# Attention pairs on one core: the second unit's normalisation after the opening, two more maximum jobs in the opening, rows loaded quad by quad

## The reference

```python
q, k, v = x @ wq.T, x @ wk.T, x @ wv.T
q, k = _apply_rope_full(q), _apply_rope_full(k)          # over the whole width
q, k, v = (t.reshape(B, S, 16, 8).transpose(0, 2, 1, 3) for t in (q, k, v))
scores = jnp.einsum('bhqd,bhkd->bhqk', q, k) / math.sqrt(8)
scores = scores + _alibi_slopes(16)[None, :, None, None] * rel[None, None]
scores = jnp.where(causal[None, None], jnp.float32(-1000000000.0), scores)
out = jnp.einsum('bhqk,bhkd->bhqd', jax.nn.softmax(scores, -1), v)
# x = x + _L0_attn_ref(_layernorm(x), ...)
```

## Time and profile before

| what | value |
| --- | --- |
| three timed runs | 1323.32, 1326.98, 1327.03 us; median 1326.98 us |
| the profiled execution: its own time | 1324.17 us |
| its span, first to last instruction | 1322.4 us |
| mean granted TensorE clock | 0.989 of full speed |

### The profile page before, as it was taken

The page is one execution under the profiler, slowest core; times in us unless marked ns, Lnnn a source line. Parts: engine busy times, 40 slices in busy tenths (PEclk is TensorE's granted clock), DMA queues, the critical chain, the costliest instruction groups (busy, mean ns, idle before and its releaser), DMA issues.

```text
span 1322.4 us, 17165 instructions
## 1 busy us (share of the span) xinstructions
PE 1220.3 (92%) x6083; PEld 784.8 (59%) x6132; DVE 906.3 (69%) x1754; ACT 641.6 (49%) x1188; POOL 241.4 (18%) x205
## 2 busy tenths in 40 slices
PE   5998788899899989899999969889998998999998
PEld 3676444567666555566667744346776665555665
DVE  6755867455467698986765677664555677889765
ACT  4544354544422597952234325454433227979222
POOL 3000100000020084751000010000000102938210
PEclk9999899999999999999999999999999999999999
DMA  6212220000101030320100032200001011212220
GB/s 231 57 33 80 56 76 19 2 1 1 64 1 64 4 118 23 116 81 1 73 25 1 24 89 54 63 3 0 1 1 64 16 50 58 81 58 80 65 72 9
DMA packets 33365, 63.27 MB, mean 48 GB/s; under 512 B 4384, under 2 KB 20096, under 8 KB 33088
## 3 DMA queue, kind: packets, MB, share of 16 engines
q1 hardware_dynamic: 33280, 62.17, 15.0%
HBM read 54.23 MB, written 8.45 MB: 47 GB/s over the span
## 4 chain that ended last, share of the span: by engine, by line
PE 72%; DVE 11%; ACT 9%; issue 3%; POOL 2%; DMA 2%; SPq 1%; another core or an unknown queue 0%; DVEq 0%; POOLq 0%; ACTq 0%
PE bank L1543 13%; PE bank L1545 13%; PE bank L1544 13%; PE bank L1722 9%; PE bank L1552 5%; DVE a_mx L1426 3%; ACT n_part L1093 3%; PE bank L1877 3%; PE bank L1621 3%; ACT n_da L1085 2%; PE bank L1787 2%; PE bank L1692 2%; POOL n_hc L840 2%; PE bank L1758 2%; PE bank L1826 1%
## 5 line engine op out<-in xcount | busy, mean ns | idle before, releaser
L1270 DVE SCALAR_TENSOR_TENSOR f_hl<-bank,f_hh 128x512 fp32r<-128x512 f32 x192 | 131.9, 689 | 130.4 <-ACT f_hh L914 129.6
L914 ACT ACTIVATE f_hh<-bank 128x512 fp32r<-128x512 f32 x192 | 115.0, 599 | 188.1 <-PE bank L1621 149.2
L980 ACT ACTIVATE m_sl<-bank 128x512 f32<-128x512 f32 x144 | 86.2, 599 | 235.4 <-PE bank L1545 233.4
L840 POOL TENSOR_TENSOR n_hc<-n_h,n_cs 128x512 f32<-128x512 f32 x128 | 160.7, 1287 | 35.3 <-DVE n_h L1514 31.1
L1543 PE MATMUL bank<-xT_h,mw_h 128*128 128x512 f32 x288 | 161.2, 560 | 3.5 <-DVEq L537 2.7
L1514 DVE TENSOR_TENSOR_SCAN n_h<-n_da,bank 128x512 f32<-128x512 f32 x128 | 149.1, 1206 | 5.1 <-PE bank L1552 2.3
L1722 PE MATMUL bank<-m_h,mw 128*128 128x512 f32 x288 | 145.6, 594 | 0.0
L1337 DVE TENSOR_TENSOR m_t<-m_sl,bank 128x512 f32<-128x512 f32 x128 | 87.9, 687 | 78.7 <-PE bank L1545 77.3
L1426 DVE TENSOR_REDUCE a_mx<-bank 128x1 f32<-128x384 f32 (+3 forms) x176 | 106.0, 638 | 39.8 <-PE bank L1828 37.4
L771 POOL TENSOR_TENSOR small<-small,half 128x4 f32<-128x4 f32 (+1 forms) x24 | 26.8, 1115 | 577.3 <-DVE small L1176 577.3
L1877 PE MATMUL bank<-n_hc,ident 128*128 128x512 f32 x256 | 131.0, 599 | 0.2
(11 more groups left out here) (248 smaller groups left out, 2331.1 us busy)
## 6 DMA issues: line engine op xcount, KB each, us to landing
n_cs<-c_dram SPq DMA_DIRECT2D x32, 512.0 KB, 3.6
m_c<-comb_dram SPq DMA_DIRECT2D x28, 512.0 KB, 5.2
stage_fw<-in_fw_dram SPq DMA_DIRECT2D x6, 512.0 KB, 6.4
stack_dram<-R SPq DMA_DIRECT2D x16, 192.0 KB, 2.8
w_stage<-in_mw_dram SPq DMA_DIRECT2D x9, 256.0 KB, 2.7
stack_dram<-R SPq DMA_DIRECT2D x16, 128.0 KB, 2.6
a_q<-stack_dram SPq DMA_DIRECT2D x4, 512.0 KB, 5.3
a_k<-stack_dram SPq DMA_DIRECT2D x8, 256.0 KB, 4.7
```

The lines of the kernel that those rows point to most:

```text
L840: n_hcs.by(nc.gpsimd.tensor_tensor(n_hc[:, i % 4, :], n_h[:, i % 4, :], n_cs[:, j % C_RING, i // 2 % 2, :], ALU.mult))
L1270: f_lo.by(V.scalar_tensor_tensor(f_h[1][:, i % 4, :], bank[:, i % 3, :], 0.0, f_h[0][:, i % 4, :].bitcast(F32), ALU.max, ALU.subtract))
```

## The change

1. `plan[-1]` takes 10 instead of 8 jobs behind `vals`: 20 of the first unit's 44 maximum jobs stand in the opening instead of 18. The first unit's remaining jobs and turns come one or two steps earlier: its turns stand at steps 3, 11 and 17 (4, 12 and 19 before).
2. The second unit's jobs run from step 20 (19 before); their last one stands in step 51 (49 before) and its turns in steps 29, 37, 45 and 51.
3. `HEAD_LAG[0]` is -4: the stages of the second unit's prologue stand two score steps later. Stages 0, 2, 4, 5 and 6 (statistics, rows, transposition, high and low part), which stood in the opening, are called behind the opening, at step 0, at step 1 and in the loop.
4. Four loads of rows, one for each quad, instead of three. Where load 0 stood, loads 0 and 1 stand.
5. GpSimd computes the second unit's inverse root after the copies of the first unit's values, not before them.

```diff
@@ -61,8 +61,8 @@
 
     plan = {step: [] for step in range(-1, 2 * NS2 + 1)}
     first, second = maxima(0), maxima(1)
-    plan[-1] = first[:NS1] + [("vals", 0, 0)] + first[NS1:NS1 + 8]
-    first = first[NS1 + 8:]
+    plan[-1] = first[:NS1] + [("vals", 0, 0)] + first[NS1:NS1 + 10]
+    first = first[NS1 + 10:]
     for step in range(2 * NS2):
         count = int(1.5 * (step + 1)) - int(1.5 * step)
         plan[step] += first[:count]
@@ -87,7 +87,7 @@
 
 
 NEXT_VALUES = 12
-NEXT_MAXIMA = [(19, 51, 1.5)]
+NEXT_MAXIMA = [(20, 52, 1.5)]
 HEADS_PLAN = heads_plan()
 
 
@@ -127,7 +127,7 @@
 HEAD_PARTS = [f"{side} {c}" for side in "qk" for c in range(3)]
 HEAD_ROTATIONS = ["first", "second", "k first", "k second"]
 HEAD_RESIDUALS = ["third", "fourth", "k rest", "k last"]
-HEAD_LAG = {0: -6, 1: 11}
+HEAD_LAG = {0: -4, 1: 11}
 KEYS_LATER = 2
 
 
@@ -441,8 +441,8 @@
         a_vok = sig("a_vok", "mha", 2)
         a_fin = sig("a_fin", "mha", 1)
         a_wr = sig("a_wr", "mha", 12, 16)
-        a_ldq = [sig(f"a_ldq_{n}", "mha", 1, 16) for n in range(3)]
-        a_ldk = [sig(f"a_ldk_{n}", "mha", 2, 16) for n in range(3)]
+        a_ldq = [sig(f"a_ldq_{n}", "mha", 1, 16) for n in range(QUADS)]
+        a_ldk = [sig(f"a_ldk_{n}", "mha", 2, 16) for n in range(QUADS)]
         a_rld = sig("a_rld", "pair", 1, 16)
         a_s1 = sig("a_s1", "mha", QUADS * NS1)
         a_m1 = sig("a_m1", "mha", QUADS * NS1)
@@ -598,7 +598,7 @@
                 sp.wait_ge(a_prt.sem, a_prt.at(k, 3 * side + 2))
                 if k % 2 == 1:
 
-                    for n in range(3):
+                    for n in range(QUADS):
                         sp.wait_ge(a_ldq[n].sem, a_ldq[n].at(k - 1, 0))
                         sp.wait_ge(a_ldk[n].sem, a_ldk[n].at(k - 1, 1))
                 for slot, n, part in PART_RUNS:
@@ -610,7 +610,7 @@
 
             def head_rows_in(k, n):
 
-                first, count = ((0, 4), (4, 2), (6, 2))[n]
+                first, count = 2 * n, 2
                 to = slice(first % 4, first % 4 + count)
                 sp.wait_ge(a_wr.sem, a_wr.at(k, 5))
                 a_ldq[n].by(sp.dma_start(a_qs[first // 4][:, to],
@@ -693,13 +693,14 @@
                     if p == 0:
 
                         sp.wait_ge(unit_done, done_before(u))
-                        head_rows_in(k, 1)
                         head_rows_in(k, 2)
+                        head_rows_in(k, 3)
                     for quad in range(QUADS):
                         if p == 0 and quad == 3:
 
                             sp.wait_ge(a_s2.sem, a_s2.at(k, NS2 // 2 - 1))
                             head_rows_in(k + 1, 0)
+                            head_rows_in(k + 1, 1)
                         sp.wait_ge(a_mok.sem, a_mok.at(k, quad))
                         if p == 1:
 
@@ -715,11 +716,11 @@
                         if p == 0 and quad == QUADS - 1:
 
                             sp.wait_ge(a_s2.sem, a_s2.at(k, 3 * STEPS_4 - 1))
-                            head_rows_in(k + 1, 1)
+                            head_rows_in(k + 1, 2)
                         if p == 1 and quad == 0:
 
                             sp.wait_ge(a_s2.sem, a_s2.at(k - 1, NS2 - 1))
-                            head_rows_in(k, 2)
+                            head_rows_in(k, 3)
                 if kind == "ffn" and u + 1 < NU and UNITS[u + 1][0] == "mha":
                     k = kth[u + 1]
                     a_rld.by(sp.dma_start(rope[:], A["rope"]))
@@ -729,6 +730,7 @@
                         sp.wait_ge(w_lo.sem, w_lo.at(0, len(SPLITS) - 1))
                     head_rows(k, 1)
                     head_rows_in(k, 0)
+                    head_rows_in(k, 1)
                 if kind == "mamba":
                     state_rows(k)
                 if u + 1 < NU and UNITS[u + 1][0] == "moe":
@@ -810,7 +812,6 @@
                     if p == 0:
                         blank(k // 2, 1)
                         a_fill.by(nc.gpsimd.memset(a_v[:, :, :, DH:32], 1.0))
-                        prologue(u + 1, "guess")
                     pool.wait_ge(a_vst.sem, a_vst.at(k, 0))
                     for n, heads in enumerate((slice(0, 12), slice(12, 16))):
                         if p == 1:
@@ -818,8 +819,7 @@
                             pool.wait_ge(a_pv.sem, a_pv.at(k - 1, (11, 15)[n]))
                         a_vok.by(nc.gpsimd.tensor_copy(
                             a_v[:, :, heads, 0:DH], a_vs[:].rearrange("p t (h d) -> p t h d", d=DH)[:, :, heads]))
-                    if p == 1:
-                        prologue(u + 1, "guess")
+                    prologue(u + 1, "guess")
                 if kind == "mamba":
                     if p == 0:
                         n_fill.by(nc.gpsimd.memset(n_xp[:, :, 0:3], 0.0))
@@ -987,7 +987,6 @@
                 if p == 0:
                     for job, x, n in HEADS_PLAN[-1]:
                         head_job(k, job, n)
-                    hand_over(u, 5)
                 for s_ in range(NS2):
                     at = NS2 * p + s_
                     w = T - s_ // 2 % NT * P
@@ -1366,17 +1365,15 @@
 
                 b = batch_of(u)
                 if p == 0:
-                    for n, (job, x, which) in enumerate(HEADS_PLAN[-1]):
+                    for job, x, which in HEADS_PLAN[-1]:
                         head_job(k, job, which, b)
-                        if n == NS1 - 1:
-                            hand_over(u, 0)
-                        if n == NS1 + 3:
-                            hand_over(u, 2)
-                    hand_over(u, 6)
+                    hand_over(u, 0)
                 V.tensor_tensor(X[:, b], X[:, b], out_b[:].unsqueeze(1).to_broadcast([P, NT, P]), ALU.add)
                 for s_ in range(NS2):
                     for job, x, which in HEADS_PLAN[NS2 * p + s_]:
                         head_job(k - p + x, job, which, b - p + x)
+                    if p == 0 and s_ == 0:
+                        hand_over(u, 2)
                     if s_ >= HEAD_LAG[p] and s_ >= 1:
                         hand_over(u, s_ - HEAD_LAG[p])
             def normalise(k, g):
@@ -1741,7 +1738,6 @@
                     ready(u)
                     for job, x, which in HEADS_PLAN[-1]:
                         head_job(k, job, which)
-                    hand_over(u, 4)
                 for s_ in range(NS2 + 3 * p):
                     at = NS2 * p + s_
                     if s_ < NS2:
@@ -1768,6 +1764,8 @@
                             head_job(k - p + x, job, which)
                     if at >= 3 and at % 2 == 1:
                         weigh_heads(k - p, (at - 3) // 2)
+                    if p == 0 and s_ == 1:
+                        hand_over(u, 4)
                     if s_ > HEAD_LAG[p] and 1 <= s_ < NS2:
                         hand_over(u, s_ - HEAD_LAG[p])
             def weigh_heads(k, tile):
@@ -1790,7 +1788,7 @@
 
             def rows_of_quads(k, n):
 
-                pe.wait_ge(a_fill.sem, a_fill.at(k // 2, 1 if n == 0 else 3))
+                pe.wait_ge(a_fill.sem, a_fill.at(k // 2, 1 if n < 2 else 3))
                 pe.wait_ge(a_ldq[n].sem, a_ldq[n].at(k, 0))
                 pe.wait_ge(a_ldk[n].sem, a_ldk[n].at(k, 1))
 
@@ -1817,8 +1815,8 @@
                 if job == "slot":
 
                     quad, (qt, h0, nh) = n // NS1, SLOTS_4[n % NS1]
-                    if n % NS1 == 0 and quad != 1:
-                        rows_of_quads(k, max(quad - 1, 0))
+                    if n % NS1 == 0:
+                        rows_of_quads(k, quad)
                     w = (qt + 1) * P
                     last = bank[:, b, 0:nh * w].rearrange("p (h w) -> p h w", w=w)[:, :, qt * P:w]
                     for c in range(nh):
```

## The result

The changed kernel takes 1330.92 us in the median of six runs (1329.63 to 1332.84); the kernel before, in its six runs, 1325.76 us (1323.32 to 1327.03). The ratio is 1.0041, 95% interval 1.0031 to 1.0051: 5.4 us slower, 4.1 to 6.8. I forecast slower by 2.4 us. The profiled execution took 1331.07 us with a span of 1329.3 us, so 6.9 us more than the one before; 1.3 us of these lie ahead of the first pair, where the two programs are the same (TensorE's last products there begin at 130.25 instead of 128.93), and are no effect of the change. (The pair's first maximum job stands at 132.76 for 131.68, 1.1 us later: the other 0.2 us are won at the pair's first load, as forecast.)

The account below looks back on a forecast made before the run. TensorE was taken as the bound (busy 92%, 72% of the chain), so only its waits in the two attention pairs pay. 2 x (2.2 - 0.9) - 0.2 = +2.4 us gave 1329.4 us on the median 1326.98; range 1322 to 1334.

Parts of the forecast that it names:

- Opening: Pair's start: step 0 begins 2.3 us earlier, at 145.0, but PE then waits 1.5 us before the transposition.
- The rows' chain: Second unit's rows: ACT's copy ends 2.3 us later, at 175.0; rows land at 184.6, 1.2 us later than before.
- step 12: End of dense steps 3 to 11: begins at 167.6, 0.2 us ahead; bounds 1.6 ahead to 0.7 behind.
- Rival D: Second unit's key load: halving it saves nothing, rows land 1.2 us later than forecast, +2.4 us, 1331.8; chance 0.10.
- What it has done ahead is that product, which before ran slow: At the wait for the second unit's rows: values product and step 20's scores already done, PE 0.9 us ahead.
- The price behind it: After the second unit's rows land: left-over jobs, waits at steps 32 and 40, later turns; 2.2 us behind per pair.
- a quad's parts fall into step 43, where the next unit's statistics begin: 0.3: Second unit's end: 1.0 us of VectorE parts of the maxima meet the next unit's statistics, costing 0.3 us.
- Quad 3's maxima: On SP's queue: they queue behind two loads and land some 2 us before step 24.
- A: The forecast itself, every step a row's duration: own range 1327 to 1332; chance 0.40.
- B: Steps 32, 40, 48, 56: PE waits 1.9, 1.3, 0 and 0.5 us for maxima rows; +6.2 us, 1333.2; chance 0.20.
- C: Second unit's rows not late: copy only 0.9 us later, PE 2.3 ahead; faster, about 1323.5; chance 0.20.
- E: Whole kernel: the change moves nothing, waits trade places one for one, 1327.0; chance 0.10.

Follow-up runs that it names:

- e8: e1 with the second unit's normalisation behind the opening, its stages two steps later and the later root (parts 3 and 5 added): 1330.42 us.
- e1: The kernel before with part 4 alone, four loads of rows, one for each quad: 1319.23 us.
- e5: The changed kernel with part 4 undone, so load 0 brings quads 0 and 1 again: 1334.77 us.
- e13: e1 with the keys' last residuals and parts two steps earlier (KEYS_LATER 0 instead of 2): 6.5 us slower than e1.
- e9: e1 with 6 instead of 8 jobs in the opening: 1331.18 us.

## Why the prediction was right in sign and too small

**Opening: right.** Step 0 at 145.0 (145.2 on before's clock), gated by the maxima rows; 1.5 us ahead of the transposition (1.48); "lent, not earned": the 1.9 and 1.5 us of step 0 have shrunk to 0.6 and 0.8 by step 16 and are worth nothing by themselves, as e8 shows.

**The rows' chain: right in kind, short by 0.9 us.** I had ACT's last part at 175.0 and it ended at 175.9; hence the landing 185.5 and not 184.6. The load was 3.47 us for 3.5 forecast, the wait of 2.37 for 2.6, the last turn's 1.92 for 1.9. The failing term is step 12, which I put 0.2 ahead of before; it began at 168.5, 0.7 behind, which was the far end that I had given for it. Rival D is out: the loads here took 3.47 us (3.21 in e1) against 4.57, and undoing the smaller loads in e5 costs 3.8 us. D rested on the fixed cost of about 2 us that the Trainium skill states, page "DMA: Bandwidth & Descriptors", section "Latency and other measured facts". The two times don't contradict such a cost, only what was concluded from it: if 256 KB take 4.57 us and 128 KB 3.47, a straight line through both leaves 2.4 us that do not shrink and 2.2 that halve (an estimate; the query load in front of the key load was halved with it, so the key load's own bytes are not tried alone).

**"What it has done ahead is that product, which before ran slow": wrong.** I counted the slow stretch behind the wait as something that the product could be moved out of. The stretch came behind the wait and then covered other work: 5.66 us at 0.50 instead of 3.2. At step 24 the first pair is 1.2 us behind where I had it 0.9 ahead with 0.5 us of jobs left over; of these 1.6 us about 0.9 are the late rows. The rest is of the size that 2.5 us more at half rate make; no run takes the stretch away by itself. In the second pair, where the stretch is as long before as after, step 24 is 1.3 us ahead, more than I had. What I had missed altogether is how much the wait was worth with its clock: e1 won 7.1 us where I expected 2.4.

**The price behind it: mis-sized in both directions.** I gave 0.5 + 1.1 + 0.5 - 0.6 us to jobs left over, steps 32 and 40 and the early turns, in sum 1.5. Steps 24 to 40 cost 0.2. The wait at step 32 was about 0.6 and at step 40 there was none; and besides the turns' 0.50 us, of which I had counted 0.3, two waits of 0.44 us (at 203.55 and 215.22 before) shrank to 0.21, at which I had not looked. Against this I gave 0.3 us to step 43 and 0.4 to the last turn, and steps 40 to 56 cost 2.6 and 3.8: the term "a quad's parts fall into step 43, where the next unit's statistics begin: 0.3" is the one that failed. VectorE there:

```profile
226.18 0.17 DVE L1433 CAST a_mp<-a_mx 128x16 bf16<-128x16 f32 x1
...
226.86 0.86 DVE L1156 BATCH_NORM_STATS2 st<-X 128x6 f32<-128x128 f32 x4
...
231.21 1.12 DVE L1185 TENSOR_SCALAR xn<-X,mv,small 128x128 f32<-128x128 f32 x4
...
237.22 0.68 DVE L1192 SCALAR_TENSOR_TENSOR xT_l<-bank,xT_h 128x512 fp32r<-128x512 f32 x1
```

Parts of the maxima until 226.35, statistics from 226.86, rows of the normalisation from 231.21 and the low part at 237.22, each ahead of a reduction that holds a bank. PE waits 1.25 us for the one, 1.16 for the next, and 0.52 for the low part, where before one wait of 1.22 us stands: 1.7 us more, and the last turn 0.7: together 2.4 of the 2.6 us of the first pair. The second pair's 1.2 us more stand beside the low clock behind the last turn. I had priced the VectorE work that is added (1.0 us of parts), and not that the jobs run two steps further into the next unit's normalisation, where each instruction of it stands between two reductions.

**Quad 3's maxima.** They queue behind two loads, as I said; I had them land some 2 us ahead of step 24. SP issued (times of the queue):

```profile
185.91 0.56 SPq L708 DMA_DIRECT2D max_dram<-R  x1
189.32 1.50 SPq L712 DMA_DIRECT2D a_q<-max_dram  x2
```

3.41 us between the write's issue and that of its loads, where a write and its wait take 1.38 us elsewhere in the same trace (202.66). The loads of the maxima rows are issued by 190.82; with the 2.04 us that such a load took at 204.82 they landed by 192.9 at the latest (an estimate), and step 24 begins at 194.85. So 2 us were left, as forecast, and PE doesn't wait there; 1.2 of them come from step 24 being late itself.

**Rivals.** A has the right places, with a wrong size at the end of the unit. B (1333.2) has nearly the right time by the wrong place: from the turn at 201.46 to the landing at 206.86 the maxima's way took 5.4 us for my 5.2, and the wait for it in the first pair is 0.6 us at step 32 and none at 40 and 56, not 1.9, 1.3 and 0.5. Its sum was wrong besides: 1.9, 1.3 and 0.5 instead of 1.1, 0.5 and 0 are 2.1 us more for each pair, not 1.3, and B would have stood at 1334.8. C is out: the chain was late by more, not less. E is out by the interval. I thought a difference too small to tell likeliest, within 4.0 us; it is 5.2 to 5.4. What carried it over that border is the end of the second unit. That the time lies within 1322 to 1334 proves little: that range holds the kernel before as well. From the first job to step 56 the pairs are 3.9 and 2.7 us longer, for 1.3 forecast.

Not settled: the clock. Low stretches come behind idle time of PE, but the wait of about 1.45 us in front of the turn of `a_o` is followed by one in e1's second pair (0.50 from 819.5 to 821.5 us) and not in its first. How much of the difference between medians it makes can be bounded, since every execution has its mean granted clock: 0.989 for the kernel before (65 executions), 0.991 for the changed kernel, 0.993 for e1, 0.990 for e13. At two levels, one half of the other, that is an estimated 28, 23, 18 and 27 us at the lower one in each execution, and each of them costs at most half its length. So the changed kernel has less of it than the kernel before, not more, and is slower for all that: its waits cost what the medians show and up to 2.5 us besides. Of e1's 7.1 us up to 5 can be the clock's, and of the 6.5 us between e1 and e13 up to 4.5.

## What to carry to other kernels

Moving work out of a stretch that waits for one engine is worth only what the next gate allows; find the chain that ends in the next long wait, and count in which step its last stage stands, before you price anything that is won in front. When jobs of one unit are pushed back, look at what the following unit has already placed there on the engine that frees the banks, instruction by instruction, not by its sum. Work that is done early is not sent early when something else stands in front of it in the queue (e9, e13). And take the parts of a change apart: here one of them was worth 7 us and the others hid it.
